# A two-layer mixture-of-experts program in two parts: linear attention with the first experts for all sixteen batches, then softmax attention with the second experts between

## The reference, cut to what matters

```python
xn = layernorm(x)
x = x + cosformer(xn) + ffn0(xn)        # layer 0
xn = layernorm(x)
x = x + softmax_attention(xn) + ffn1(xn)  # layer 1

# cosformer, 16 heads of 8: q, k = relu(xn @ W + b); each times sin and cos of the position
kv = einsum('nld,nlm->ndm', k_, v);  z = 1 / max(q_ . sum(k_), 1e-4);  out = (q_ @ kv) * z @ Wo + bo
# ffn0: 2 shared and 16 routed experts of width 64, gelu, the best 4 gates of a softmax
# softmax attention, 16 heads of 8: rope, causal mask, softmax(q k / 11.3) @ v @ ow
# ffn1: 8 experts of width 512, only the best one per token
h = x @ w1[e]; a, g = split(h); y = (silu(a) * g @ w2[e]) * max_prob
```

## Time and profile before

| | |
|---|---|
| median of 3 runs | 1344.12 us (1340.39 to 1346.58) |
| the profiled execution's own time | 1337.22 us |
| its span, first to last instruction | 1335.4 us |
| busy: PE, DVE, ACT, POOL | 1201.5, 962.6, 945.2, 682.3 us |
| mean granted TensorE clock | 0.961 |

### The profile page before, as it was taken

One profiled execution on the slowest core, in us unless ns is written; L12 is line 12 of the kernel. 1 busy time (PEld: TensorE's weight loads), 2 busy tenths in 40 slices (PEclk: granted clock), 3 DMA queues, 4 the chain that ended last, 5 costly groups with the idle time before them and its releaser, 6 DMA issues.

```text
span 1335.4 us, 28936 instructions
## 1 busy us (share of the span) xinstructions
PE 1201.5 (90%) x9960; PEld 696.8 (52%) x9960; DVE 962.6 (72%) x2450; ACT 945.2 (71%) x1312; POOL 682.3 (51%) x933
## 2 busy tenths in 40 slices
PE   5877989989999999999999999999987878779996
PEld 3433343444454544545454545545433556679996
DVE  5437585888888988888888888888768553346664
ACT  3224777868797888888897888888765646546663
POOL 3452536464847566574847575574854212323333
PEclk9887999999999999999999999999986988999998
DMA  4650505141433416061532325060734311112222
GB/s 142 157 116 21 106 15 112 37 102 40 99 77 57 104 31 127 7 129 30 109 69 65 95 40 122 12 128 15 157 123 94 98 29 29 39 45 72 72 70 45
DMA packets 85502, 101.46 MB, mean 76 GB/s; under 512 B 11734, under 2 KB 63062, under 8 KB 85096
## 3 DMA queue, kind: packets, MB, share of 16 engines
q1 hardware_dynamic: 77904, 86.44, 28.9%
q0 software_dynamic: 7456, 13.19, 3.5%
HBM read 73.68 MB, written 25.90 MB: 75 GB/s over the span
## 4 chain that ended last, share of the span: by engine, by line
PE 72%; ACT 10%; DVE 8%; issue 5%; POOL 5%; DMA 0%; ACTq 0%; DVEq 0%; POOLq 0%
PE PS L734 10%; PE PS L701 10%; PE PS L537 9%; PE PS L585 8%; PE PS L668 6%; PE PS L686 5%; PE PS L516 4%; PE PS L745 4%; ACT flow L846 3%; ACT qp L837 3%; PE PS L529 3%; PE PS L551 2%; POOL early L1258 2%; PE PS L652 2%; PE PS L718 1%
## 5 line engine op out<-in xcount | busy, mean ns | idle before, releaser
L846 ACT ACTIVATE flow<-PS 128x1024 f32<-128x1024 f32 x320 | 320.3, 1023 | 93.8 <-PE PS L686 90.0
L1271 POOL TENSOR_SCALAR_AFFINE_SELECT flow<-flow 128x256 f32<-128x256 f32 (+1 forms) x448 | 191.3, 442 | 301.1 <-ACT flow L846 299.6
L701 PE MATMUL PS<-flow 128*32 128x512 f32 (+3 forms) x2048 | 181.1, 455 | 3.8 <-POOL flow L1271 2.3
L1101 DVE TENSOR_REDUCE nm<-PS 128x2 f32<-128x1024 f32 x128 | 154.6, 1218 | 38.7 <-PE PS L652 38.7
L1258 POOL TENSOR_TENSOR early<-early 128x512 f32<-128x512 f32 x128 | 164.7, 1303 | 3.0 <-DMA early<-gate_rows 2.5
L837 ACT COPY qp<-PS 2x512 f16<-2x512 f16 x256 | 147.5, 576 | 18.6 <-PE PS L676 15.0
L1304 POOL DMA_INDIRECT out_y<-ysb,rowu x72 | 70.9, 985 | 169.4 <-DVE rowu L1209 162.4
L585 PE MATMUL PS<-early,down 128*128 128x512 f32 x288 | 150.4, 626 | 6.3 <-POOL early L1258 5.0
L537 PE MATMUL PS<-xnT,up 128*128 128x512 f32 x288 | 147.9, 630 | 8.6 <-DVE rb L1045 2.7
L668 PE MATMUL PS<-kp,qp 34*128 34x512 f16 (+3 forms) x1024 | 125.4, 309 | 32.6 <-ACT flow L846 16.4
L1103 DVE TENSOR_REDUCE nm<-PS 128x2 f32<-128x768 f32 x128 | 121.4, 948 | 41.9 <-PE PS L652 40.6
(11 more groups left out here) (169 smaller groups left out, 2202.3 us busy)
## 6 DMA issues: line engine op xcount, KB each, us to landing
early<-gate_rows SPq DMA_DIRECT2D x64, 512.0 KB, 8.2
qp<-relay_q SPq DMA_DIRECT2D x64, 128.0 KB
kp<-relay_k SPq DMA_DIRECT2D x64, 128.0 KB
xsb<-xs SPq DMA_DIRECT2D x72, 65.0 KB, 1.9
x2g<-x SPq DMA_DIRECT2D x72, 64.0 KB, 1.9
relay_k<-qkh SPq DMA_DIRECT2D x32, 128.0 KB
early<-in_w SPq DMA_DIRECT2D x1, 4096.0 KB, 13.0
relay_q<-qkh SPq DMA_DIRECT2D x16, 128.0 KB, 9.4
```

Source lines behind the costliest of these rows:

```text
L701: ins = pe.matmul(m.PS[32 * j:32 * j + 32, m.PV, kt * P:], m.vst[b % 2][:, kt, 4 * g + j, :], m.pt[:, r, k * L + o:k * L + o + L - kt * P] ...
L846: act.activation(m.pt[:, n % RING, :], m.PS[:, i:i + 2, :].rearrange("p k c -> p (k c)"), ACT.Exp, scale=1.0 / SCALE).then_inc(s["exp"], 1)
L1101: dve.tensor_reduce(nm[:, 3, :, n], ps, AX_X, ALU.max, negate=True).then_inc(s["max"], 1)
L1271: ins = pool.affine_select(part, part, [[0, part.shape[1]], [1, P]], ALU.is_ge, nothing, base=0, channel_multiplier=-1)
```

## The change

Layer 0 and all preparation of layer 1 are now done for all batches first (`FIRST + SECOND`, 20 numbers per batch); softmax attention is a second series that begins at `A0 = S1 * B - 40` = 280, that is when batch 14 is at number 0, and six tiles stand inside each batch of attention from the third on. There is one tile less (71). What this takes:

- Two sets of layer 0's buffers, used by even and odd batches (the second set lies in memory that attention uses later: its exp buffers and the second q/k buffer). The last two batches both use the first set (`side_of`, `before`).
- q, k and v of all batches wait in DRAM (`relay` has a batch dimension, `values` is new: `vout`, `vload`, `vst`).
- The rows of maxima: one fp32 transpose per group of heads in the place of four fp16 ones, one ACT and one DVE instruction on 16 rows, and two small DMAs (`mlow` on SP) in the place of four ACT copies.
- `kv` as 16 small matmuls of 32 output rows and 66 columns in the place of 8 of 129 columns; sin and cos are multiplied into v on ACT and not into k on DVE; the layer norm's normalization moves from DVE to ACT; `gT` is one transpose and not four.
- The tiles' stores hold the expert's part alone. The sum of x and attention is added by 16 accumulating stores (`add` on POOL), for all batches and not for the last two, after all tiles' stores have landed. The indirect stores of x to sorted places (`sort2`, 64 of them) and the tiles' loads of them (`x2g`) are gone.
- `score` uses a ring of 6 exp buffers (was 4), and `value` has 2 groups of 5 units (was 3).

```diff
-NTILE = B * NT + E1
-RING = 4
+NTILE = B * NT + E1 - 1
+RING = 6
-VALUES = {1: (0, 1), 3: (2, 3), 4: (4,)}
+VALUES = {1: (0, 1), 4: (2, 3, 4)}
+S1, S2 = 20, 20
+A0 = S1 * B - 40
-LAST += [(tile(n) + 0.05, "load", n + U) for n in range(NTILE - U)]
+TPB, TB0 = 6, 2
+TILES = placed(
+    tile=[24.25, 24.85, 28.5, 29.3, 35.65, 36.3])
+def tile(n):
+    return S2 * (TB0 + n // TPB) + TILES[n % TPB][0]
...
-    out = [(NS * b + at, name, b, i) for b in range(B)
-           for at, name, i in (OPENING[b] if b < len(OPENING) else FIRST + SECOND + ATTENTION)]
+    out = [(S1 * b + at, name, b, i) for b in range(B)
+           for at, name, i in (OPENING[b] if b < len(OPENING) else FIRST + SECOND)]
+    out += [(A0 + S2 * b + at, name, b, i) for b in range(B) for at, name, i in ATTENTION]
     out += [(at, name, 0, i) for at, name, i in START]
-    out += [(NS * (B - 1) + at, name, 0, i) for at, name, i in LAST]
+    out += [(A0 + at, name, 0, i) for at, name, i in END + LAST]
...
+def side_of(b):
+    return b % 2 if b < B - 2 else 0
+def before(b):
+    return b if b == B - 1 else b - 1
...
     def mrows(b, g):
-        pe.wait_ge(s["mparts"], b * G + g + 1)
-        ps = bank(("mrows", b, g)).bitcast(F16)
-        for t in range(NT):
-            ins = pe.transpose(ps[:, t * P:(t + 1) * P], m.mt[:, g % 2, t, :], m.identh[:, :])
-        ins.then_inc(s["m_mm"], 1)
+        pe.wait_ge(s["max"], (b * G + g + 1) * NU)
+        ps = bank(("mrows", b, g))
+        nm = m.nm[:, g % 2, :, :, :].rearrange("p k x t -> p (k x t)")
+        pe.transpose(ps[0:4 * NT, 0:P], nm, ident).then_inc(s["m_mm"], 1)
...
+    def mlow(b, g):
+        sp.wait_ge(s["mlow"], b * G + g + 1)
+        for r in range(2):
+            sp.dma_start(m.qp[b % 2][MROW + r::64, 2 * g:2 * g + 2, :], m.mrows[:, g % 2, r, :]).then_inc(s[f"d_mrows{g % 2}"], 16)
...
+    def add(_, b):
+        if b == 0:
+            for u in range(U):
+                pool.wait_ge(s[f"d_ys{u}"], 16 * ((NTILE - u + U - 1) // U))
+        pool.wait_ge(s["x2"], b + 1)
+        pool.dma_start(m.out_d[:, b], m.X[:, b * NT:(b + 1) * NT, :], accum_op=ALU.add).then_inc(s["d_out"], 16)
```

More of the change, by code:

```diff
@@ L151 @@
-ATTENTION = placed(
[L152 to L163, removed]
@@ new lines @@
+    gate=[-16.95],
+    attn0=[-8.2],
+    gT=[-9.2],
+    at0T=[-7.35])
+SECOND = placed(
+    down=[-3.45, -2.15, -1.4, -0.35, 1.45, 2.3, 3.9, 4.35, 6.3],
+    gated=[-5.55, -5.05, -3.25, -3.2, -1, -0.5, -0.25, 0.2],
+    x1=[7.45],
+    stats1=[8.45],
+    norm1=[12.55],
+    xnT1=[12.6],
+    rope=[14.45, 22.35],
+    parts=[18.55, 31.2],
+    v=[15.8],
+    logits=[13.2],
+    route1=[13.25],
+    expert=[15.8],
+    ranks=[17.75],
+    sort=[17.35, 18.35, 20.25, 20.8],
+    vout=[22.85])
@@ new lines @@
+OPENING = [placed(
+    stats0=[-500.8],
+    norm0=[-481.85],
+    xnT0=[-470.55],
+    kvr=[-464.25, -463.7, -461.05, -444],
+    up=[-462.8, -457.8, -456.95, -436.15, -386.4, -303.8, -249.65, -189.2, -144.05],
+    q=[-426.65],
+    kv=[-263.35],
+    route0=[-257.95],
+    gate=[-240.35],
+    attn0=[-212.75],
+    gT=[-210.75],
+    at0T=[-205],
+    down=[-177.75, -177.15, -176.45, -170.65, -158.15, -145.2, -143.55, -142.1, -142.05],
+    gated=[-407.85, -403.35, -401.85, -401.8, -391.8, -381.5, -380.95, -380.5],
+    x1=[-62.7],
+    stats1=[-61.45],
+    norm1=[-35.2],
+    xnT1=[-21.1],
+    rope=[-13.35, 12.45],
+    parts=[-2.25, 18.25],
+    v=[3.5],
+    logits=[-2.45],
+    route1=[-1.1],
+    expert=[-0.1],
+    ranks=[2.5],
+    sort=[-11.4, 20.15, 21.65, 24.95],
+    vout=[-142.85])]
@@ new lines @@
+ATTENTION = placed(
+    score=[28.65, 29.35, 29.4, 33.1, 33.8, 35.1, 35.25, 35.7, 36.05, 36.35, 36.65, 38.45, 40.85, 42.6, 44.3, 44.45,
+           45, 45.45, 47.05, 47.4],
+    max=[17.2, 18.05, 20.6, 22.3, 23.5, 23.55, 24.5, 25.55, 28, 28.25, 28.4, 28.9, 29.05, 29.6, 30.05, 31, 33.3,
+         34.05, 35.3, 36],
+    mrows=[26.7, 29.85, 35.15, 37.45],
+    mlow=[27.1, 31.1, 35.15, 38.05],
+    value=[33.1, 35.2, 37.35, 39.5, 43.5, 45.8, 47.4, 50.3],
+    sums=[41, 51.5],
+    heads=[42.75, 53.85],
+    mT=[59.85],
+    out=[61.55],
+    relay=[7.15],
+    vload=[11.85],
+    vst=[29])
@@ L282 @@
     "gT": ("gT", 1), "at0T": ("at0T", 1), "x1": ("x1", 1), "xnT1": ("xl", 1), "logits": ("logits", 1),
[L283 removed]
+    "rope": ("rope", 2), "v": ("vcopy", 1), "heads": ("heads", 2), "ranks": ("base", 1), "mrows": ("mlow", G), "mT": ("mT", 1), "out": ("x2", 1),
 }
@@ L584, in down @@
             pe.wait_ge(s["gated"], b * (NC - 1) + c)
-        pe.matmul(m.acc, m.down[:, c, :], m.hid[:, c, :], start=(c == 0), stop=False)
+        pe.matmul(m.acc, m.down[:, c, :], m.hid[side_of(b)][:, c, :], start=(c == 0), stop=False).then_inc(s["read"], 1)
         if c == NC - 1:
@@ L1323, in fill @@
             ins.then_inc(s["fills"], 1)
-    share = dict(fill=fill, stats0=stats0, stats1=stats1, q=q, gated=gated, score=scores, rope=rope, sort=sort, sort2=sort2,
-                 outputs=outputs)
+    share = dict(fill=fill, stats0=stats0, stats1=stats1, q=q, gated=gated, score=scores, rope=rope, sort=sort, add=add,
+                 rows=rows, outputs=outputs)
     nothing = pool.to_reg(0.0)
```

492 lines of the change are left out of this document (207 added, 285 removed).

## The result

The changed kernel takes 1429.89 us (median of 4, 1425.18 to 1438.94) against 1345.35 us (median of 4): a ratio of 1.064, 95% interval 1.058 to 1.070. I had predicted 1264, faster. The profiled execution took 1430.85 us, its span 1429.1: 172 us more than the sum of 1257.

What follows compares the result with a forecast made beforehand. PE, 90% busy, was taken to bound the kernel, with 166 us lost outside steady work. Work of 1134 us plus 40, 10, 21, 10, 27 and 15 gave a 1257 us span, hence 1264 us predicted, range 1235 to 1290.

Steps and rivals of the forecast that it cites:

- the sum of 1257: Whole kernel: predicted span in us, PE's remaining work plus all allowances for idle time and lost clock.
- PE's work left, 1134 us: Whole kernel: PE's steady work after 32 us saved over 16 batches and one tile less.
- the 1169: Kernel before: PE's steady work in us, 16 batches at 60.5 and 72 tiles at 2.79.
- First part, +10: Layer 0 and preparation: PE needs some 31 us a batch, plus 0.7 a batch for waits attention had hidden.
- the paragraph on the shared port: First part: DVE and POOL lock each other out; six waits of half 1.3 us could cost 4 us a batch, +60.
- First rival, the gates' loop: First part: the loop through gates' DMA and POOL takes 35 us a batch, 1320 us in all; chance 0.17.
- Attention without tiles, 37 us a batch, +27: Attention at beginning and end: two score-bank pairs bound it, 9 us a batch for 2.5 batches, 5 us more at the beginning.
- The fourth rival, half clock: Attention without tiles: PE mostly at 1.2 GHz, 40 us more, 1305 us; chance 0.12.
- Transition, priced at nothing: Between first part and attention: no cost allowed; a stall there, waiting for batch 14's buffers, would make the prediction wrong.
- Tiles as filling: Attention with six tiles: 28 us and 16.7 make 45 us a batch; switches add 21 in all, late rows 10.
- Start, +40: Beginning: 25 us idle PE and 5 us lost clock as before, plus 10 as batch 1 waits for batch 0's rope.
- Second and third rival: Second: maxima rows' DMA comes late, 1351 us and over, chance 0.10. Third: all waits are covered, 1212 us, chance 0.18.

Runs made afterwards that it cites:

- fills: Changed kernel with POOL's gate products in batches 0 to 13 replaced by about equally long fills that read nothing: 1401 us (1.043 to 1.056).
- the kernel without gating: Changed kernel without the products by the gates, POOL only signalling: 1371 us (1.022 to 1.026).
- third pair at the end: Changed kernel with gate products on DVE, plus banks 5 and 6 as a third score-bank pair after the last tile: 1377 us (1.024 to 1.038).
- tiles spread: Changed kernel with gate products on DVE, plus the 71 tiles spread over attention batches 2 to 15, five in most: 1410 us (1.041 to 1.054).

## Why the prediction was wrong

- *PE's work left, 1134 us*: not refuted, but the wrong frame. With the lock gone the first part shows the 31 to 32 us a batch I had counted. The sum allowed 123 us for idle PE and lost clock together; idle time alone is 213 us. Busy time is 82 us above the 1134, where before it was 33 above the 1169 counted the same way; the lower clock is in that, how much isn't shown.
- *First part, +10*: the term that failed most, 54 us. I had the mechanism, in the paragraph on the shared port, with six instructions waiting half of 1.3 us, and I put it at 4 us a batch in a rival at 0.17 under another name. Measured: six kinds of DVE products (`e`, two of `rk`, `ohb`, `oh`, `qkl`) are 0.5 to 1.0 us longer on average than with fills (`qkl` by two of 20 that are held for 4.6 us), and PE loses 3.4 us a batch, with the lower clock in it; by the fills that is 41 of the 54 us, by the kernel without gating 50. I excused it by 5 us of cover that `expert` to `ranks` doesn't have once attention is away: PE waits 1.9 us there.
- *First rival, the gates' loop*: its 35 us a batch came true for the wrong reason. After the start `down` does not wait for POOL, and fills as long as the gates run 3.4 us a batch faster.
- *Attention without tiles, 37 us a batch, +27*: mis-sized twice. It takes 45 to 47 us at the end: I priced holding a pair (1.7 and 1.45 us) and 0.1 us for handing over. Over the 80 uses from 1282 to 1377 us after, the mean of maxima and scores is 1.99 and 1.59 us from PE's first matmul to the reader's end, and a pair then stands empty for 0.61 us until PE, in its fixed order, comes round: (1.79 + 0.61) x 40 / 2 = 48 us. That is bookkeeping, since in strict turn hold and empty time always add up to the period; that the pairs bound is shown by the third one, 41.3 us for 46.8. The fourth rival, half clock, is real (0.79 and 0.80 in batches 14 and 15), but hardly lengthens the holding: with tiles, at a clock of 1.00 (800 to 1200 us), the same means are 1.94 and 1.58 us. My single pair of the earlier trace rows was a short one. What half clock costs otherwise is not shown.
- *Transition, priced at nothing*: the sentence that would make me wrong did. 36 us over plan. DVE's tables take 13 us there, of which 7 are shown to lie on the path; the share of half clock (0.67) stays open, as do the 13 us ahead of the first maxima.
- *Tiles as filling*: with tiles a batch takes 48.8, not 47.1. That six tiles fit in beside attention was right; that they determine its time was not, as five take 48 too.
- *Start, +40*: 12 us more; PE waited once 9.2 us for ACT's normalized rows and once 8.0 for POOL's gated block. Not tested.
- *Second and third rival*: late rows of maxima cost 2.3 us in ten batches; nothing was covered. (The third's 1212 also takes 17 and 4 us where the terms were 27 and 10; with these it would be 1196.)

So the step that failed is the first part's term: the lock between DVE and POOL was priced at nothing in the sum, as covered, and it costs 41 to 50 us, the lower clock beside it included. The pairs of banks, the transition and the tiles were sized too low by 21, 36 and 26 us, only in part explained.

## What to carry to other kernels

Before a slow engine-to-engine product is put beside a chain of small ones, look at which of them read two SBUF tensors: if DVE and POOL both do, price each of DVE's at up to a whole POOL instruction (here 0.5 to 1.0 us of 1.27 on average), and watch for one that waits through several in a row (here twice, 5.3 us through four), unless other work covers it; and don't take one-input copies and scalings on DVE as free of it. Work that is split into phases loses what each phase hid in the other, so price each phase alone, by its longest chain of waits and not by the busiest engine's sum. And a handful of buffers used in strict turn by an in-order engine has a period of hold plus the time until that engine comes round; measure both on a stretch where nothing else runs.

## What the runs showed that I had not expected

- The same first part, with the same waits, runs at 31.6 to 32.8 us a batch in one execution and at 33.6 on average in another. Windows at 150 to 500 us of two kernels whose programs agree there, third pair at the end and tiles spread:

```profile
150.00:500.00 350.00, 317.34 (x1654) 173.31 (x1653) 253.75 (x912) 241.96 (x458) 143.54 (x173) 0.98 0.43 105
```

```profile
150.00:500.00 350.00, 318.66 (x1561) 177.56 (x1560) 243.03 (x874) 233.34 (x438) 139.91 (x171) 0.91 0.41 101
```

  PE is as busy, runs 6% fewer instructions and is granted 0.91 and not 0.98. The second one changes on its way: its periods are 31 to 33 us for batches 1 to 5 and 34.0 to 34.1 from batch 6 on:

```profile
90.00:250.00 160.00, 143.44 (x723) 76.89 (x722) 108.92 (x395) 104.64 (x199) 61.71 (x76) 0.98 0.41 98
...
300.00:500.00 200.00, 183.01 (x879) 102.22 (x878) 137.56 (x491) 132.30 (x249) 79.76 (x96) 0.90 0.39 97
```

  What decides it stays open.
- A DVE instruction with one SBUF tensor and a scalar for each partition (normalization, 128x128) is locked out by POOL as well: 3.14 us for four, against 1.11. A one-input CAST of 128x4 is held even by a POOL fill that reads nothing: 855 ns on average, against 163.
- A DVE product that needs 0.69 us (`qkl`) twice took over 5 us, beside four of POOL's gate products in a row; 18 others took 0.69.
- 40 useless matmuls a batch raised the granted clock from 0.79 to 1.00, and the batch took 42.6 us instead of 41.2.
- DVE's 128x32 product `p` stays at 1.06 us in all of these kernels: it stands beside POOL's rope addition, which also reads SBUF and which no run moved.
